# Loads of x moved from the SP queue to the ScalarE queue in a pre-norm attention and LoRA-expert layer on eight cores

## The reference

```
x = x + attn(layernorm(x), Wq, Wk, Wv, Wo)     # 32 query heads, 8 key/value heads, head size 128
                                               # rotary embedding on q and k, causal softmax
x = x + ffn(layernorm(x), A, B, Wr)            # 4 experts of rank 16, gate: softmax over the best 2
```

## Time and profile before

| | us |
|---|---|
| profiled execution, time | 4264.28 |
| profiled execution, span of the slowest core | 4262.7 |
| spans of the eight cores | 4216.9 to 4262.7 |
| other runs, lowest and highest | 4253.01, 4568.32 |
| median shown | 4410.67 |
| TensorE busy | 3217.9 (75%) |
| VectorE busy | 1164.8 (27%) |
| ScalarE busy | 900.8 (21%) |

### The profile page before, as it was taken

One profiled execution on the slowest core, in us unless ns is written; L12 is line 12 of the kernel. 1 busy time (PEld: TensorE's weight loads), 2 busy tenths in 40 slices (PEclk: granted clock), 3 DMA queues, 4 the chain that ended last, 5 costly groups with the idle time before them and its releaser, 6 DMA issues.

```text
span 4262.7 us, 46120 instructions; the slowest of 8 cores (4216.9 to 4262.7 us)
## 1 busy us (share of the span) xinstructions
PE 3217.9 (75%) x17520; PEld 1512.0 (35%) x17520; DVE 1164.8 (27%) x2613; ACT 900.8 (21%) x917; POOL 72.7 (2%) x86
## 2 busy tenths in 40 slices
PE   3656666666537998789539998879736999887983
PEld 1222223222213444434214444434313444443441
DVE  3111106100253223410462222220254221212016
ACT  2000004000111004700211006820012003983001
POOL 0000000000000000000000000000000000000000
PEclk9888887788757999989759999989857999998995
DMA  7999991898534552044144550024223552002431
GB/s 161 184 178 185 192 186 32 187 179 171 113 125 138 168 176 80 5 164 148 40 177 142 170 173 26 1 107 150 99 119 133 170 176 85 1 1 84 154 119 79
DMA packets 215705, 530.64 MB, mean 124 GB/s; under 512 B 82112, under 2 KB 168256, under 8 KB 169408
## 3 DMA queue, kind: packets, MB, share of 16 engines
q1 hardware_dynamic: 53280, 421.72, 27.4%
q0 software_dynamic: 87456, 84.97, 15.3%
q10 hardware_dynamic: 74752, 20.99, 2.4%
HBM read 474.19 MB, written 117.44 MB: 139 GB/s over the span
## 4 chain that ended last, share of the span: by engine, by line
PE 57%; DMA 17%; DVE 12%; ACT 9%; issue 5%; DVEq 0%; ACTq 0%; SPq 0%; POOLq 0%
PE pd L293 47%; ACT epair L577 8%; DMA wblk<-wq 5%; DMA wblk<-wo 5%; DVE bst L333 4%; PE pd L612 3%; PE pd L319 3%; PE pd L553 3%; DMA wblk<-wscr 1%; DMA wblk<-wv 1%; DMA h<-x 1%; DVE epair L589 1%; DMA wblk<-wk 1%; DVE hnT L303 1%; DMA wscr<-wblk 1%
## 5 line engine op out<-in xcount | busy, mean ns | idle before, releaser
L293 PE MATMUL pd<-xnT,wblk 128*128 128x512 bf16 x5120 | 1154.1, 389 | 155.8 <-DMA wblk<-wq 127.5
L293 PE MATMUL pd<-wblk,aoT 128*128 128x512 bf16 x4096 | 926.9, 390 | 155.3 <-DMA wblk<-wo 119.2
L293 PEld LDWEIGHTS pd<-xnT,wblk 128*128 128x128 bf16 x5120 | 508.6, 100 | 800.4 <-issue 230.7
L577 ACT ACTIVATE epair<-pd,cvals 128x1024 bf16<-128x1024 f32 x544 | 629.5, 1201 | 323.9 <-PE pd L553 279.5
L293 PEld LDWEIGHTS pd<-wblk,aoT 128*128 128x128 bf16 x4096 | 408.2, 100 | 673.1 <-issue 219.0
L612 PE MATMUL pd<-vaug,epair 128*128 128x129 bf16 x4352 | 355.5, 222 | 164.2 <-ACT epair L577 95.5
L319 PE MATMUL pd<-iden,xnhn 128*128 128x128 bf16 x1024 | 144.4, 301 | 390.7 <-ACT xnhn L349 349.3
L612 PEld LDWEIGHTS pd<-vaug,epair 128*128 128x128 bf16 x4352 | 265.3, 98 | 415.9 <-issue 410.0
L366 DVE TENSOR_TENSOR t1b<-qswp,sing 128x512 bf16<-128x512 bf16 x160 | 110.8, 693 | 1067.5 <-DMA qswp<-qt 889.4
L695 DVE TENSOR_TENSOR h<-pd,h 128x512 f32<-128x512 f32 x128 | 79.5, 684 | 1007.3 <-PE pd L293 1007.3
L337 ACT ACTIVATE lnv<-agg,cvals 128x1 f32<-128x1 f32 x32 | 9.4, 295 | 1516.4 <-DVE agg L335 1516.4
(11 more groups left out here) (55 smaller groups left out, 920.2 us busy)
## 6 DMA issues: line engine op xcount, KB each, us to landing
wblk<-wscr SPq DMA_DIRECT2D x240, 1024.0 KB, 5.5
wscr<-wblk SPq DMA_DIRECT2D x80, 1024.0 KB, 7.9
h<-x SPq DMA_DIRECT2D x24, 2048.0 KB, 11.0
wblk<-wq POOLq DMA_DIRECT2D x32, 1024.0 KB, 15.7
wblk<-wo POOLq DMA_DIRECT2D x32, 1024.0 KB, 14.5
out<-h SPq DMA_DIRECT2D x16, 2048.0 KB, 6.6
qswp<-qt ACTq DMA_DIRECT2D x256, 64.0 KB, 5.0
wblk<-wk POOLq DMA_DIRECT2D x8, 1024.0 KB, 13.2
```

The source lines that it names most:

```text
L293: nc.tensor.matmul(o, l, r, start=st, stop=sp))
L577: nc.scalar.activation(epair[p][:, 0:ncols], src, AF.Exp, bias=cvals[:, 3:4], scale=cvals[:, 2:3]))
```

## The change

1. The loads of x, in A (L417, 16 of them) and in D (L671, 8 of them), are issued with `sch.Z` on ACT's queue in place of `sch.X` on SP's. Their place in the source is unchanged, and so is what they wait for: the load of a tile in A stands directly ahead of that tile's layer norm.
2. Both tables of the rotary embedding are now waited for, not only the second; in groups after the first the second load repeats the waits of the first. The first product of `rope` on DVE (L366) takes the waits for the tables too.
3. Each transpose waits for `iden`.

```diff
@@ transpose_tile
-                w = ready_fn(ci)
+                w = ready_fn(ci) + [iden_ready]
@@ rope
-        v1 = sch.V([z1, z2, ("A", prod)] + wq0,
+        v1 = sch.V([z1, z2, ("A", prod)] + wq0 + waits,
@@ start
-    tb = sch.X([], lambda e: e.dma_start(cosg[:, :], cost_d[:, 0:512]))
-    tb = sch.X([], lambda e: e.dma_start(sing[:, :], sint_d[:, 0:512]))
-    rg_tab.use(*tb)
+    tb1 = sch.X([], lambda e: e.dma_start(cosg[:, :], cost_d[:, 0:512]))
+    tb2 = sch.X([], lambda e: e.dma_start(sing[:, :], sint_d[:, 0:512]))
+    rg_tab.use(*tb1)
+    rg_tab.use(*tb2)
@@ A, per tile
-            xv = sch.X(wts, lambda e, r=row0, s=slot: e.dma_start(h[s][:, :],
+            xv = sch.Z(wts, lambda e, r=row0, s=slot: e.dma_start(h[s][:, :],
                                                                   x_d[r:r + 128, :]))
@@ B
-        wtab = [tb]
+        wtab = [tb1, tb2]
@@ after B
-            sch.X([lastrope] + wt, lambda e, gg=g + 1: e.dma_start(
+            tb1 = sch.X([lastrope] + wt, lambda e, gg=g + 1: e.dma_start(
                 cosg[:, :], cost_d[:, gg * 512:(gg + 1) * 512]))
-            tb = sch.X([], lambda e, gg=g + 1: e.dma_start(
+            tb2 = sch.X([lastrope] + wt, lambda e, gg=g + 1: e.dma_start(
                 sing[:, :], sint_d[:, gg * 512:(gg + 1) * 512]))
-            rg_tab.use(*tb)
+            rg_tab.use(*tb1)
+            rg_tab.use(*tb2)
@@ D, tiles 0 and 1
-                xdma[jl] = sch.X(wts, lambda e, r=row0, jl=jl:
+                xdma[jl] = sch.Z(wts, lambda e, r=row0, jl=jl:
                                  e.dma_start(h[jl][:, :], x_d[r:r + 128, :]))
```

## The result

The changed kernel is faster by about 1%: ratio 0.9906 of its times to those of the kernel before, 95% interval 0.9877 to 0.9935. The profiled execution took 4215.3 us (span 4213.8) where that of the kernel before took 4264.3. (Some executions of either kernel run up to 9% longer, at a lower clock on one die or both, and so did the traced one of the experiment that moves only the loads of A; the median shown ahead is shifted by these, the ratios leave them out.)

A forecast was written before the change was run, and what follows sets the result against it. The prediction took TensorE's projections and weight transfers to bound the kernel, with SP's queue held by x loads. Its terms, -34.3 - 5 - 40.4 + 48 + 21.6 = -10.1 us, took 4264.3 to 4254 us, range 4225 to 4298.

The forecast's parts named there:

- Step 1: Attention into output projection, groups 1 to 3: Wo blocks no longer stand behind held x loads on SP; gain 34.3 us.
- The copies in group 0: Output projection of group 0: weight copies to scratch made during attention, so the third Wo block goes earlier; gain 5 us.
- Step 2: End of a group into the next layer norm: first x load issued earlier on ACT; gain 40.4 us.
- The cover of the first evacuation: Layer norm start: the fourth store lands 1.5 us before the first evacuation into xnT, which overwrites h0 and h1.
- Step 3: Inside the layer norm, groups 1 to 3: loads on ACT lose their lead, tiles 19.6 us apart; cost 48 us.
- "add 2": Layer norm, groups 1 to 3: 2 us added because the second tile's load meets the fourth store and two Wq blocks.
- Group 0 in A: Layer norm of group 0: x loads take turns with computation and share DMA engines with weight loads; cost 21.6 us.
- the projections don't win it back: Group 0's q/k/v projections: the stage moves whole, so the layer norm's added 21.6 us is not recovered.
- Free edits: Added waits for iden, the second table and on L366: covered by earlier waits; 0 to 1 us together.
- Rival (a): Nine single layer-norm loads land more slowly, making the kernel slower; at 10.8 us each, 11 us worse, 4275; chance 0.2.
- the 1.5 us of the prediction: Start of the layer norm, groups 1 to 3: wait left per group for the first x load beside a store.

The follow-up runs named there:

- the lead experiment: Changed kernel with layer-norm x loads of tiles 0 and 1 issued first, tile jl+2 behind the L349 activations of tile jl; ratio 0.9845 to the kernel before.
- The experiment with the added wait: Changed kernel with layer-norm x loads of tiles 1 to 3 also waiting for the last L349 activation of the tile before; ratio 0.9996 to the kernel before.
- the last version: Changed kernel with the next group's first two x loads issued at the previous group's end, later loads leading, first evacuation waiting only for h0's store; ratio 0.9826 to before.

## Why the prediction was wrong, step by step

- **Step 1, into D: right.** Forecast 34.3, measured 32.1 on the mean of the cores; the slowest core, which the prediction had read, went from 35.3 us of idle time to 1.2. With the load of D alone, the same 32 to 33. D's first matmul follows the last transpose by 0.33 to 0.46 us.
- **The copies in group 0: the mechanism is seen, the size is open.** The third Wo block went out 4.1 us sooner, where 4.8 was forecast. D of group 0 scatters by 11 us between executions, so the 5 us can't be read from its length.
- **Step 2, from E into A: right, 7 us too hopeful.** The wait on VectorE went from 41.3 us in three places (mean of the cores) to 8.2. That is 33.1 gained for a forecast of 40.4. Half of the gap is that the prediction read the slowest core, where the wait was 44.9; the other half is the wait left, 2.7 us each and not 1.5, since the load landed in 12.5 us. The cover of the first evacuation held (8.79 us behind the statistics as before), and failed at once when two loads were put ahead (the lead experiment).
- **Step 3, inside A: this is the step that failed.** The prediction put each load behind "the four L349 activations of the tile before": 6.58 + 4.64 + 0.25 + 8.1 = 19.6. The second term is not there. The queue issues at 6.58 + 0.2, and for tiles 2 and 3 that gives 6.8 + 8.1 = 14.9, or 14.58 where the landing is shorter; measured 15.1 and 14.8. Tile 1 came out as forecast, 19.4, but for another reason: its landing was 12.5 us, behind two Wq blocks and a store, which was the "add 2" of the prediction and should have been more. In sum the nine tiles cost 16.4 us and not 48. The experiment with the added wait gives back what the prediction had: 20.0, 19.4, 19.3.
- **Group 0 in A.** Forecast +21.6, measured +9.7, for the same term: with the wait, 98.5 us for a forecast of 98.3. (Its bounds were added up wrong: 10 for the second load and 7.6 for the others give +15, and 14.5 for the third gives +27, where it has +14 and +28. Neither reaches +9.7.) That "the projections don't win it back" was right, though the first pair of traces seemed to say otherwise.
- **Free edits: right**, 1.0002.
- **The sum.** With the 5 us of the copies left as forecast, the errors are 31.6 us in step 3 and 11.9 in group 0, less 7.3 in step 2 and 2.2 in step 1: 34 us, from -10.1 to -44, where the ratio gives about -40. The range did not reach there because no bound was put under the term that was wrong. The place of the load was treated as known from the source. No row of before shows when ACT issues a DMA that has nothing to wait for: the DMAs of `rope` all wait for the activation just ahead of them. So the term was unknown, 0 to 4.64 us twelve times, and stood in no bound: up to 56 us. The rivals were all about the landing. Rival (a) had something in it for tile 1 alone.
- The rule of the Trainium skill that was held against the change ("DMA: Bandwidth & Descriptors", Rules for kernel authors: issue early, compute, wait late) was right in its sign: both versions that issued the loads of x earlier have a shorter A. The waits inside A are the cost of the short lead, and the last version has none of them in groups 1 to 3. It is not the whole story, since holding the Wq blocks back gained 12 us as well.

## What to carry to other kernels

A DMA that moves to the queue of a computing engine should be costed from when that queue can issue it, which is when its own waits and those that stand ahead of it in the list are met, and not from the end of the work ahead of it. For the same reason its place in the source does not protect what that work still reads: a DMA that overwrites it needs a wait. Where the trace has no such DMA, the whole of that work is a bound, not a term. When a held queue is set free, ask what it now sends early and whose transfer that meets. And a stage that is bound by transfers shared between cores scatters more than such a change is worth, so read the gain from stages that repeat, and test a suspected absorption by a delay too large to be scatter.

## What the runs showed of the hardware

- A DMA on ACT was issued 0.10 to 0.21 us after the start of the first of four activations ahead of it, with 4.4 to 4.5 us of them still to run; with a semaphore wait on the fourth it came 0.08 to 0.19 us behind its end (96 loads in each trace). The Trainium skill ("Advanced Engine Details and Errata", Sequencer Loop) says that an engine's sequencer pushes an engine instruction into a queue and starts a control instruction itself. These rows agree with it: the issue of the load did not wait for the three activations queued ahead of it.
- Two transfers on two queues share. The first load of a group landed in 12.5 us beside a store (lone: 7.6 to 8.7), and the fourth store took 9.5 us with one load ahead on the other queue and 14.7 with two, where on SP's queue alone it had taken 7.6 (means of the cores). What the prediction took from the Trainium skill ("DMA: Bandwidth & Descriptors", Queues, rings and completion order), that a DMA engine serves its queues in turn, fits; the 1.5 us of the prediction did not, since a wait of 2.7 was left, between 1.5 for sharing and 4.8 for following.
- B of group 0 (DMA engines 0.92 to 0.93 busy in the two stage tables) took 545 to 565 us in nine traces for the same work, one trace for each kernel, where B of the later groups took 335 to 337.
